# Order of the first loads and place of one centring step in a two-layer sequence kernel

## The reference

```
x = layernorm(x + gated_recurrence(x))   # causal conv of 4 taps; r, i = sigmoid(x_conv @ W.T + b)
                                         # a = sigmoid(log_a) ** (8 r); b = sqrt(1 - a*a) * i * x_conv
                                         # h_t = a_t h_(t-1) + b_t; rmsnorm(h @ out_w.T) * norm_w
x = layernorm(x + relu(x @ W1 + b1) @ W2 + b2)          # 256 -> 1024 -> 256
x = layernorm(x + ssm(x))                # in_proj, conv of 4 taps, silu, 16 states per channel,
                                         # h = exp(dt A) h + dt B x; y = sum(h C); y * silu(z) @ out_proj.T
x = layernorm(x + relu(x @ w1 + b1) @ w2 + b2)
```

## Time and profile before

| | |
|---|---|
| median of 3 runs | 956.32 us |
| profiled execution, its own time | 953.83 us |
| its span, first to last instruction | 952.0 us |
| TensorE matmul busy | 792.9 us, 83% |
| VectorE busy | 786.3 us, 83% |
| ScalarE busy | 673.2 us, 71% |
| GpSimd busy | 586.6 us, 62% |
| mean granted TensorE clock | 0.914 of full |

### The profile page before, as it was taken

One profiled execution on the slowest core, in us unless ns is written; L12 is line 12 of the kernel. 1 busy time (PEld: TensorE's weight loads), 2 busy tenths in 40 slices (PEclk: granted clock), 3 DMA queues, 4 the chain that ended last, 5 costly groups with the idle time before them and its releaser, 6 DMA issues. The chain is left out here.

```text
span 952.0 us, 9608 instructions
## 1 busy us (share of the span) xinstructions
PE 792.9 (83%) x2802; PEld 530.0 (56%) x2802; DVE 786.3 (83%) x993; ACT 673.2 (71%) x1345; POOL 586.6 (62%) x488
## 2 busy tenths in 40 slices
PE   2285866988988899999999999998997797588685
PEld 2164643746565656475647564756475556356464
DVE  5425677486799999999999999999999999999750
ACT  4348687399768867997799779867976785474542
POOL 0203447448747786788678867886787577556431
PEclk9597977989998899999999999999999998799597
DMA  8100000000100010001000100010000000000000
GB/s 316 36 1 22 23 1 22 1 1 0 57 1 0 1 56 1 0 1 67 1 1 1 61 1 0 1 45 0 1 1 28 1 1 0 22 1 1 22 1 22
DMA packets 10340, 19.49 MB, mean 20 GB/s; under 512 B 1456, under 2 KB 5296, under 8 KB 10288
## 3 DMA queue, kind: packets, MB, share of 16 engines
q1 hardware_dynamic: 10288, 18.88, 5.9%
HBM read 14.69 MB, written 4.19 MB: 20 GB/s over the span
## 5 line engine op out<-in xcount | busy, mean ns | idle before, releaser
L384 POOL TENSOR_TENSOR y<-y,hC 128x1024 f32<-128x1024 f32 (+3 forms) x140 | 270.9, 1935 | 63.2 <-DVE hC L1475 58.9
L1916 PE MATMUL pC<-w,hT 128*128 128x256 f32 x1024 | 232.9, 382 | 4.4 <-ACT hT L777 4.3
L842 ACT ACTIVATE dA<-dt,A_neg 128x512 f32<-128x512 f32 (+3 forms) x320 | 185.6, 629 | 51.8 <-DVE hs L1464 51.6
L1916 PEld LDWEIGHTS pC<-w,hT 128*128 128x128 f32 x1024 | 193.5, 191 | 38.8 <-issue 6.3
L1464 DVE TENSOR_TENSOR_SCAN hs<-dA,carry,pS 128x512 f32<-128x512 f32 (+3 forms) x192 | 193.5, 1008 | 11.8 <-DVE pS L1449 4.0
L2039 PE MATMUL pS<-stack,sel 97*128 97x512 f32 (+3 forms) x320 | 151.7, 526 | 45.4 <-DVE hs L1464 45.3
L1449 DVE TENSOR_TENSOR pS<-u,pS 128x1024 f32<-128x1024 f32 (+3 forms) x160 | 159.6, 997 | 28.3 <-PE pS L2039 27.5
L1475 DVE TENSOR_TENSOR hC<-hs,pS 128x1024 f32<-128x1024 f32 (+3 forms) x160 | 158.0, 987 | 10.9 <-PE pS L2039 10.6
L1464 DVE TENSOR_TENSOR_SCAN hs<-dA,pS 128x512 f32<-128x512 f32 (+1 forms) x128 | 138.4, 1082 | 13.7 <-POOL carry L402 4.6
L777 ACT ACTIVATE hT<-pA,ffb_sb 128x512 f32<-128x512 f32 (+3 forms) x160 | 94.3, 597 | 64.0 <-PE pA L1909 63.7
L1909 PE MATMUL pA<-tg,w 128*128 128x512 f32 (+3 forms) x320 | 124.9, 538 | 5.2 <-ACT hT L777 4.8
(11 more groups left out here) (120 smaller groups left out, 1114.4 us busy)
## 6 DMA issues: line engine op xcount, KB each, us to landing
xt<-xT SPq DMA_DIRECT2D x6, 515.0 KB, 4.7
xtok<-x SPq DMA_DIRECT2D x6, 512.0 KB, 5.1
out<-x3b SPq DMA_DIRECT2D x6, 512.0 KB, 3.0
w<-w1a SPq DMA_DIRECT2D x1, 1024.0 KB, 8.3
w<-w2a SPq DMA_DIRECT2D x1, 1024.0 KB, 10.4
w<-w1b SPq DMA_DIRECT2D x1, 1024.0 KB, 8.3
w<-w2b SPq DMA_DIRECT2D x1, 1024.0 KB, 9.9
xt<-xT SPq DMA_DIRECT2D x2, 259.0 KB, 7.8
```

Of the source, the lines that this page charges most:

```text
L384: nc.gpsimd.tensor_tensor(y[:, :, 0:ch.T], so_far, hC[:, n % CRING, :, 0:ch.T], ALU.add).then_inc(S["y_sum"], 1)
L842: nc.scalar.activation(dA[:, k % ARING, 0:ch.T], dt[ch.side][:, h, 0:ch.T], ACT.Exp, scale=A_neg[:, h, n:n + 1]).then_inc(S["dA_ready"], 1)
L1916: mm = nc.tensor.matmul(dst[:, b * D:b * D + D], src(k, t0), w[:, k, :], start=k == 0, stop=k == nk - 1)
```

## The change

1. par has a semaphore of its own, `par_loaded`, and is the only load ahead of the first chunk's xt. ffb and rows are issued behind the gate weights. ScalarE and VectorE wait at their head for par alone, POOL for none of the loads. Waits for ffb and rows (`small_loaded`, now 32) stand at their first readers: centre_b2, rms_residual of chunk 0 and the first relu of chunk 0.
2. centre_w2_0 of the first FFN's W2 moves on the VectorE from ahead of clip_log_decay to behind the recurrence of chunk 0.
3. The order functions are split further (`filling`, `second`, `ending` are new), with their conditions resolved. Written out turn by turn, every engine's sequence of calls is the one of before, but for the move of point 2. The long rest of the diff is this and is not shown.

```diff
         def _(sp):
-            for src, dst in ((par, par_sb), (ffb, ffb_sb)):
-                sp.dma_start(dst[:], src[:]).then_inc(S["small_loaded"], 16)
-            sp.dma_start(rows_sb[:], rows.rearrange("(o a) d -> o a d", o=1).to_broadcast([P, 3, D])).then_inc(S["small_loaded"], 16)
+            sp.dma_start(par_sb[:], par[:]).then_inc(S["par_loaded"], 16)
...
                 weight("gate", gate_w[:], gateT)
+                sp.dma_start(ffb_sb[:], ffb[:]).then_inc(S["small_loaded"], 16)
+                sp.dma_start(rows_sb[:], rows.rearrange("(o a) d -> o a d", o=1).to_broadcast([P, 3, D])).then_inc(S["small_loaded"], 16)
                 weight("out", out_w[:], outT)
...
             pool.wait_ge(S["eps_ready"], 2)
-            pool.wait_ge(S["small_loaded"], 48)
...
             def rms_residual(ch):
                 c = ch.i
                 pool.wait_ge(S["o_scaled"], BLOCKS[c + 1])
+                if c == 0:
+                    pool.wait_ge(S["small_loaded"], 32)
...
         def _(act):
-            act.wait_ge(S["small_loaded"], 48)
+            act.wait_ge(S["par_loaded"], 16)
...
             def relu(layer, ch, f, before=None):
+                if ch.i == 0 and layer == 0 and f == 0:
+                    act.wait_ge(S["small_loaded"], 32)
...
         def _(dve):
-            dve.wait_ge(S["small_loaded"], 48)
+            dve.wait_ge(S["par_loaded"], 16)
...
             def centre_b2(ch):
                 if ch.i == 0:
-                    centre(S["small_loaded"], 48, lambda k: rows_sb[:, 1 + k, :], 2, 0, S["b2_centred"])
+                    centre(S["small_loaded"], 32, lambda k: rows_sb[:, 1 + k, :], 2, 0, S["b2_centred"])
...
             def opening(ahead, gate, prep, scan, tail):
                 if gate is not None:
                     centre_b2(gate)
-                    centre_w2_0(gate)
                     clip_log_decay(gate)
                     log_A(gate)
                     a2_minus_1(gate)
                     gate_input(gate)
                     scaled_input(gate)
                     recurrence(gate)
+                    centre_w2_0(gate)
                     row_stats(gate)
                     row_moments(gate)
```

More of the change, by code:

```diff
@@ L212, in build, with steps @@
         block = ctx.enter_context(nc.Block())
-        def steps(opening, entry, step, closing):
+        def steps(opening, filling, entry, second, step, closing, ending):
             def chunk(i):
@@ L222, in steps @@
                 if gate is None and i > 0:
-                    part = closing
+                    part = closing if prep is not None else ending
                 elif scan is None:
-                    part = opening
+                    part = opening if prep is None else filling
                 elif scan.i < ENTRY:
-                    part = entry
+                    part = entry if tail is None else second
                 part(ahead, gate, prep, scan, tail)
@@ new lines, in opening, with filling @@
+                conv_add(ahead, 2)
+                conv_add(ahead, 3)
+            def filling(ahead, gate, prep, scan, tail):
+                row_scales(LN_PREP, prep)
+                decay_steps(gate)
+                inv_rms(gate)
+                rms_residual(gate)
+                gate_scales(gate)
+                conv_add(ahead, 1)
+                add_bias(LN_GATE, 0, x1, x1b, S["x1b_ready"], gate)
+                save_carry(prep, 0)
+                save_carry(prep, 1)
+                sum_states(prep, 1)
+                conv_add(ahead, 2)
+                save_carry(prep, 2)
+                conv_add(ahead, 3)
+                sum_states(prep, 2)
+                save_carry(prep, 3)
+                sum_states(prep, 3)
+                save_carry(prep, 4)
@@ L646, in closing @@
                     save_carry(scan, 15)
-            steps(opening, entry, step, closing)
+            steps(opening, filling, entry, second, step, closing, ending)
         @block.scalar
@@ L1201, in closing @@
-                if prep is not None:
-                    mconv_first(prep, tail)
+                x3_channel_major(tail, 0, gate)
+                x3_channel_major(tail, 1, gate)
                 if scan is not None:
                     state_decay(scan, 7)
-                if prep is not None:
-                    mconv_tap(prep, 1)
-                if scan is not None:
                     state_decay(scan, 8)
-                if tail is not None:
-                    relu(1, tail, 0, prep)
@@ L1236, in closing @@
+                relu(1, tail, 6)
+                relu(1, tail, 7)
                 if scan is not None:
@@ new lines, in opening, with filling @@
+                conv_early(ahead)
+            def filling(ahead, gate, prep, scan, tail):
+                centre_b2(gate)
+                centre_w2_0(gate)
+                centre_op(prep)
+                centre_w2_1(prep)
+                history(prep)
+                add_ffn0(prep, 0, tail)
+                clip_log_decay(gate)
+                log_A(gate)
+                a2_minus_1(gate)
+                gate_input(gate)
+                scaled_input(gate)
+                recurrence(gate)
+                z_silu(prep, 0)
+                z_silu(prep, 1)
+                mconv_early(prep)
+                mconv_silu(prep)
+                x_proj_low(prep)
+                row_stats(gate)
+                row_moments(gate)
+                dt_x(prep)
+                state_input(prep, 0)
+                state_scan(prep, 0, 0)
+                state_scan(prep, 0, 1)
+                state_input(prep, 1)
+                state_scan(prep, 1, 0)
+                state_output(prep, 0)
+                state_scan(prep, 1, 1)
+                state_input(prep, 2)
+                state_scan(prep, 2, 0)
+                state_output(prep, 1)
+                state_scan(prep, 2, 1)
+                state_input(prep, 3)
+                conv_early(ahead)
+                state_scan(prep, 3, 0)
+                state_output(prep, 2)
+                state_scan(prep, 3, 1)
+                state_input(prep, 4)
+                state_scan(prep, 4, 0)
+                state_output(prep, 3)
+                state_scan(prep, 4, 1)
+                state_input(prep, 5)
@@ new lines, in closing, with ending @@
+                state_scan(scan, 14, 0)
+                x_proj_low(prep)
+                if tail.nj == 2:
+                    add_ffn1(tail, 1)
+                state_output(scan, 13)
+                state_scan(scan, 14, 1)
+                state_input(scan, 15)
+                state_scan(scan, 15, 0)
+                state_output(scan, 14)
+                dt_x(prep)
+                state_input(prep, 0)
+                state_scan(scan, 15, 1)
+            def ending(ahead, gate, prep, scan, tail):
@@ L1891, in closing @@
                     state_output(scan, 14)
-                if prep is not None:
-                    dt_x(prep)
-                    state_input(prep, 0)
-                if scan is not None:
                     state_scan(scan, 15, 1)
-            steps(opening, entry, step, closing)
+            steps(opening, filling, entry, second, step, closing, ending)
         @block.tensor
@@ L2244, in entry, with filling @@
                     down(0, gate, 0, 0, tail=tail)
                     down(0, gate, 0, 1)
-                if scan is not None:
-                    spread_C(scan, 15)
+            def filling(ahead, gate, prep, scan, tail):
+                gate_mm(gate, 0, 0)
+                gate_mm(gate, 0, 1)
+                gate_mm(gate, 1, 0)
+                gate_mm(gate, 1, 1)
+                x2_transpose(prep, 0, gate)
+                x2_transpose(prep, 1, gate)
+                in_proj_x(prep, 0)
+                in_proj_x(prep, 1)
+                in_proj_z(prep, 0, tail)
+                in_proj_z(prep, 1, tail)
+                out_proj0(gate, prep)
+                x_proj(prep, tail)
+                dt_row(prep)
+                spread_B(prep, 0)
+                spread_B(prep, 1)
+                x1_transpose(gate, 0, prep, tail)
+                x1_transpose(gate, 1, prep, tail)
+                up(0, gate, 0)
+                up(0, gate, 1)
+                spread_C(prep, 0)
+                spread_B(prep, 2)
+                up(0, gate, 2)
+                up(0, gate, 3)
+                up(0, gate, 4)
+                up(0, gate, 5)
+                spread_C(prep, 1)
+                up(0, gate, 6)
+                up(0, gate, 7)
+                spread_B(prep, 3)
+                spread_C(prep, 2)
+                down(0, gate, 0, 0, tail=tail)
+                spread_B(prep, 4)
+                spread_C(prep, 3)
+                down(0, gate, 0, 1)
+                spread_B(prep, 5)
@@ L2461, in closing @@
                     spread_C(scan, 14)
-                if prep is not None:
-                    spread_B(prep, 0)
-                if scan is not None:
                     spread_C(scan, 15)
```

(2 more changed lines are left out.)

1498 lines of the change are left out of this document (774 added, 724 removed).

## The result

| | before | changed |
|---|---|---|
| median | 955.11 us (6 runs, 953.61 to 956.44) | 948.07 us (6 runs, 944.06 to 949.0) |
| profiled execution, its own time | 953.83 us | 947.77 us |
| its span | 952.0 us | 946.0 us |

The account below looks back on a forecast made before the run. Engines' instruction chains, released by semaphores, were taken to bound the kernel, so the head's gain reaches the end. Centring 3.39 plus loads 2.03 less POOL 0.10 gave 5.3 us: 956.32 to 951.0 us, range 948.7 to 953.6.

Parts of the forecast that it names:

- What bounds it, and that the head's gain arrives: Semaphore-released middle from 100 to 900 us: a head over d us sooner makes the end d us sooner.
- The first part's size: Loads at the head: xt lands 4.5 us after issue, first tap at 5.73 instead of 7.76, 2.03 us sooner.
- rival A: Head loads: xt lands at 3.87, before the ScalarE is free at 4.40; gain 6.65 us, time 949.7; chance 0.10.
- Rival B: Head loads: xt still lands near 7.7 though issued first; only the centring counts, time 953.0; chance 0.06.
- That the loads alone bring nothing and the centring alone 3.4: At the clip: W2's landing held it at 20.48 whenever x came; the centring's share of the gain is 3.39 us.
- The cover of 3.7 us: VectorE behind the recurrence: centring runs to about 30.7, row_stats is wanted at 34.4; each us past costs one.
- Rival C: Behind the recurrence: centring becomes the bound of row_stats, ending 3.1 us late; gain 2.2 us, time 954.1; chance 0.05.
- The 0.1 us for POOL: At rms, beside the last of the centring's eight subtractions: POOL loses 0.1 us, between 0 and 0.55.
- The clock, held to be a rare spoiler: TensorE's granted clock: no term in the sum, only in two rivals, chances 0.07 and 0.03.
- rival E: Up and down projections wholly at the lower TensorE clock: 13.1 us more, time 964.1; chance 0.03.
- Rival D: Shifted head or last stages: another TensorE clock takes 3 to 5 us of the gain, time 954.5 to 957; chance 0.07.
- The range: Whole kernel's time: 948.7 to 953.6 us, each end widened by 1.0 us for the spread of the runs.

Follow-up runs that it names:

- run 5: Changed kernel with 8 unused VectorE statistics between clip and scan of chunk 0 as an added delay: 949.61 us, against 947.46 without.
- run 6: Changed kernel with 16 unused VectorE statistics between clip and scan of chunk 0 as an added delay: 951.74 us, against 947.46 without.
- run 8: Changed kernel with gate weights and all later loads issued only once the first chunk has landed: 948.51 us, a single execution.
- run 10: Changed kernel with the chunk issued ahead of par, the logarithm behind the convolution, and 20, 40 and 46 unused matmuls in TensorE gaps: 942.82 us.
- run 3: Changed kernel with ffb and rows issued between par and the first chunk again, ScalarE and VectorE still waiting for par alone: 951.18 us.
- run 1: Changed kernel with the centring put back ahead of the clip, so only the loads and waits are changed: 954.77 us, ratio 1.0006 to before.
- run 2: Changed kernel with the loads and waits of the kernel before, so only the centring is moved: 951.41 us, ratio 0.9967 to before.
- run 4: Changed kernel with the centring of out_proj and the second FFN's W2 also moved behind the recurrence, ahead of row_stats: 952.46 us.
- run 9: Changed kernel with the chunk issued ahead of par and the decay constant's logarithm behind the convolution: 948.06 us, ratio 0.9931 to before.
- run 11: As run 10, but only 15 unused matmuls ahead of the gates and an unread 2-column tanh behind the logarithm: 943.09 us.

## Why the prediction was off, point by point
- **What bounds it, and that the head's gain arrives: right, to about 1 us.** The medians of runs 5 and 6 and the shift of 6.1 us at the last sum for 6.6 at chunk 0's show it; a single execution can lose 2 us more behind the head (runs 6, 8, 10).
- **The first part's size: wrong, and this is the step that failed.** I took 4.5 us for the landing of xt, midway between rows_sb's 3.5 and xt's own 5.6. It is 3.1 to 3.8. The 5.6 was no bound of the new case but a measurement of the old one: runs 3 and 8 show that some 2.4 us of it were the rows ahead. The term was 3.38 us and not 2.03 in the profiled execution, where rival A (0.10) came true: the chunk landed at 4.27, later than A's 3.87 but still ahead of the constants, and the tap at 4.38 was bound by them; in the six other traces with this queue the tap waited 0.20 to 0.69 us for the chunk and started at 4.71 to 5.10. So the term is 2.7 to 3.4 us, and the first tap lay between the forecast's 5.73 and rival A's 4.40, nearer to A. The gain by medians, 5.9 to 7.0 us, lies on both sides of A's 6.65. Rival B is out by run 1's tap.
- **That the loads alone bring nothing and the centring alone 3.4: right** (runs 1 and 2: gains of 0.1 and 3.5 us by medians).
- **The cover of 3.7 us: right** (3.92 left, run 4). Rival C did not occur.
- **The 0.1 us for POOL: too much where I put it, and the wrong place to look.** rms took 0.71 us as before, though its first 0.38 us lay beside the last subtractions (until 28.79), so neither the 0.1 nor the 0.55 of the upper bound came. Where a POOL operation on full tiles meets the VectorE the price is real: 1.0 us in run 4, 0.60 in runs 5 and 6. The row that I read as a loss of 0.84 us for the VectorE alone also was a stroke of luck for the chain, since it was not POOL that waited.
- **The clock, held to be a rare spoiler, is in every run.** In the profiled execution the gates won 0.41 us on the path and up lost 0.53. The 7.18 us at the clip are 3.38 + 3.39 + 0.41; less 0.53 at up and 0.55 behind chunk 0's sum (0.4 of it between chunk 1's sum and chunk 2's) they leave 6.1 at the last sum. These terms were not in my sum: that the profiled execution came within 0.7 us of its forecast is in part luck, since a load term 1.35 us too small and 1.08 us lost later cancel in part. Of rival E's 13.1 us 0.5 came, at up; down stayed at full clock. Rival D's 3 to 5 us did not come.
- **The range: too narrow below.** It took A's full gain from a median of three runs that lay 1.2 us above that of six. Single runs of the kernel before lay between 950.7 and 956.8 us within one session, 6 of 35 under 951.2 and none between 951.2 and 952.9. All six have a mean granted clock of 0.919 and the other 29 have 0.905 to 0.917; the changed kernel's fastest run, 944.06, has 0.920 and its other five 0.912 to 0.917. So the low runs go with a higher clock; where in the execution and why is open, since no trace is of such a run.

## What to carry to other kernels
A load's time to landing holds what was ahead of it (here 2.4 us of 5.5). To price a new order, look for a load of like size with the new case's queue ahead, and don't average it with the old case. Two waits that end near each other hide each other's gains: do the arithmetic of each part alone and of both, and expect the sum only where each is last in turn. Where TensorE runs short bursts with idle time between, its clock is a term of the sum (here 4.5 us of 948), and matmuls on nothing can buy it back.

## What the runs showed that I had not expected
- Which of VectorE and POOL waits for the other can't be read from the start times. In the changed kernel POOL shows 15.40 and the VectorE 15.46, and the VectorE is the long one (1.53); in run 5 POOL shows 17.67 and the VectorE 17.73, and POOL is the long one (1.64). The Trainium skill, page "SBUF — State Buffer", section "Who interferes with whom", says that the later one waits for the whole of the other; the sizes agree (0.60 is within 0.1 of the VectorE's 0.69), the order of the recorded starts doesn't tell it.
- A small subtraction (128x256, one tensor input) also waited for POOL: 1.62 us for 0.62 in run 4.
- A ScalarE table load can stand ahead of the semaphore wait of the operation that needs it (5.49 in the changed kernel) or behind it, on the chain (10.41 in run 9, 10.27 in run 10). An earlier small operation with the same function took it along (7.10 in run 11).
- Gate weights of 512 KB issued 2.4 us later were still in time.
